# A decoder layer's seam between two attentions: the second one's first projections and norms issued in the first one's last slots

## The chip, the core and the metric

The kernel runs on one core of a Trainium2 chip. The metric is the device time in microseconds (us) of one execution of the whole program. TensorE (PE) multiplies, with PEld its weight loads; VectorE (DVE), ScalarE (ACT) and GpSimd (POOL) work on elements; SyncE (SP) issues most transfers. Each engine runs its own instructions in order, and the engines are tied together by semaphores.

## The reference

Three blocks, each followed by a norm over the 256 columns. B = 4 batches, S = 512 rows, C = 256.

```python
x = layernorm(x + attn(x))      # 16 heads of 64, softmax(q k^T / 8 + bias[bucket(k - q)]) v, then @ o_w.T
x = layernorm(x + xattn(x, ctx))
x = layernorm(x + ffn(x))       # x + sum over the 3 best of 8 zones of gelu(x @ Wa) @ Wb * w

def xattn(x, ctx):              # 16 heads of 16
    q, k, v = heads(x @ Wq + bq), heads(x @ Wk + bk), heads(x @ Wv + bv)
    y = softmax(where(causal, q k^T * scale, -inf)) v
    qc, kc, vc = heads(x @ Wcq + bcq), heads(ctx @ Wck + bck), heads(ctx @ Wcv + bcv)
    y = y + softmax(qc kc^T * scale) vc
    return y @ Wp + bp
def layernorm(x): return (x - mean(x)) / sqrt(var(x) + eps)
```

## The kernel before

Most products are made of two float16 halves of each factor (xhi + xlo, whi + wlo), as three products that add up in one bank: high by high, low by high, high by low. So every projected or turned matrix leaves its bank twice: ScalarE writes the high half and VectorE subtracts it from the bank for the low half.

**attention_1** works on 32 units u, a pair of heads of one batch each (8 pairs, 4 batches, the batch outermost). It is written as a pipeline of slots t = 0..36, each with four quarters i = 0..3. In slot t unit t is projected (project_qk, project_v, lines 371 and 381), unit t−1's row maxima are taken (line 394 on TensorE, 686 on VectorE), unit t−2's and t−3's scores are made (416, 417), get their position bias from VectorE (695) and their exponential from ScalarE (574), and are multiplied by v (426). GpSimd adds the exponentials up (768) and splits the sums (low_sum, 773); TensorE sums them over the rows (sums, 441). Unit t−4 is projected out, a quarter of the rows at a time (project_out, 458): VectorE adds the first head's part to x_acc (add_out, 715), ScalarE weighs the second head's (weigh, 595), and GpSimd adds that (add_out, 780). project_out of the next quarter waits for VectorE's addition and ScalarE's weighing. In slots 6 and 10 ScalarE and VectorE also split weights of the second attention (524 and 653). In slot 35 TensorE turns the four contexts (turn_context, 467), and in slot 36 the normalised batch 0 (turn_first, 475).

**The norm** is the class Norm: statistics (lines 140 to 145, VectorE), root (150, ScalarE, which needs a table load), even (155 to 160, VectorE: reciprocal, shift and tiles 0 and 2) and odd (166, ScalarE: tiles 1 and 3). For batch 0 it runs in slots 34 and 35, for the others in the second attention.

**attention_2** has 16 units of four heads (4 groups, 4 batches) of both the causal and the cross attention. Its order is a clock n, with tables that say at which n a unit's step stands: unit u's maxima at n = 16 + 16u + i (i = 0..15), scores from 38, values products (pv) on even n from 42, and so on. The steps overlap: at one n the maxima of one unit, the scores of the one ahead, the pv of another and the projections of the next are issued. Before the change the clock starts at n = −16. A unit's q and k (self), and on even u the cross q and on odd u the cross k for a pair of units, are projected into bank_a (line 914), in two halves on two neighbouring steps:

```python
u, i = unit_at(n, CROSS, 2)          # CROSS = -12: i = 4 and 5 of the unit whose maxima are taken
if u is not None and (u % 2 == 0 or i == 0):
    project_cross(u, i)
u, i = unit_at(n, SELF, 2)           # SELF = -5: i = 11 and 12
if u is not None:
    project_self(u, i)
```

ScalarE (high_self, high_cross) and VectorE (low_self 1177, low_cross 1183) write the halves, SyncE stores them to HBM and moves them back in eight transfers (901 to 907), so that each head lies in its place in q and k. VectorE takes the maxima from two banks (1194), four reductions to a step, and TensorE fills the banks (990, 996), scores (1020) and pv (1038). Norms and turns of batches 1 to 3 and the value products of all batches (VALUES) stand at n = −11 to 27.

## Time and profile before

| | us |
|---|---|
| median of three runs | 1324.45 |
| the three runs | 1322.35 to 1327.92 |
| the profiled execution | 1322.84 |
| its span | 1321.1 |
| mean granted TensorE clock | 0.965 |

| engine | busy us | share of the span |
|---|---|---|
| TensorE | 1182.4 | 89% |
| VectorE | 915.6 | 69% |
| ScalarE | 830.9 | 63% |
| GpSimd | 479.5 | 36% |

The busy shares are means over stages. attention_1 ends at about 566 us, attention_2's projections and norms of the first unit fill the time to 598, its units follow up to about 980, and the third block closes the span. The granted clock is a share of full speed.

### The profile page before, as it was taken

Reading aid. Unit: us, or ns where it says so; the run is one execution under the profiler, and the core shown is the slowest. Engines: PE = TensorE matmul, PEld = TensorE weight load, DVE = VectorE, ACT = ScalarE, POOL = GpSimd, SP = SyncE. Lnnn points to the kernel's source line nnn. Section 1 sums busy time; section 2 is a strip of 40 time slices with the busy share of each in tenths; the row PEclk is TensorE's granted clock in tenths of the full one; section 3 lists DMA queues with packets and bytes.
Section 4 is the critical chain, followed back from the end, with each engine's and each line's share of the span. In section 5 each row is a group of like instructions: output and inputs, shape, how many; then the busy total and the mean of one; then the engine's idle time right before and its main releaser. Section 6 shows DMA issues by size and latency. Waiting matters only on the chain. (4 is left out here: it accounts for less than half of the span.)

```text
span 1321.1 us, 25115 instructions
## 1 busy us (share of the span) xinstructions
PE 1182.4 (89%) x8862; PEld 549.9 (42%) x8862; DVE 915.6 (69%) x2346; ACT 830.9 (63%) x1587; POOL 479.5 (36%) x511
## 2 busy tenths in 40 slices
PE   6799999999999999768988888988887279999998
PEld 2343434444444444243222232222225246666666
DVE  3777777777777777557787888878842765656564
ACT  3566666666666666542667677677773476666663
POOL 0267777788888878821111111111220000000000
PEclk9999999999999999888799999999999689999999
DMA  7543324323332232011211211212100083232100
GB/s 218 164 119 100 99 77 116 83 82 82 82 91 79 78 84 57 2 54 55 70 52 41 73 50 51 72 47 67 33 2 0 5 316 121 87 128 82 63 17 16
DMA packets 82482, 103.00 MB, mean 78 GB/s; under 512 B 12626, under 2 KB 74066, under 8 KB 82326
## 3 DMA queue, kind: packets, MB, share of 16 engines
q1 hardware_dynamic: 81334, 101.26, 26.0%
q8 instruction: 71, 1.16, 0.4%
q14 instruction: 53, 0.43, 0.1%
q0 software_dynamic: 1024, 0.13, 0.1%
HBM read 65.37 MB, written 10.68 MB: 58 GB/s over the span
## 5 line engine op out<-in xcount | busy, mean ns | idle before, releaser
L1194 DVE TENSOR_REDUCE a_mx<-a_m 128x1 f32<-128x512 f32 (+3 forms) x512 | 269.0, 583 | 71.0 <-PE a_m L990 63.0
L1128 ACT ACTIVATE a_pt<-a_s 128x512 f32<-128x512 f32 (+3 forms) x512 | 235.3, 515 | 85.5 <-PE a_s L1020 82.4
L574 ACT ACTIVATE a_pt<-a_s 128x512 f32<-128x512 f32 x256 | 149.5, 597 | 164.6 <-DVE a_s L695 137.8
L990 PE MATMUL a_m<-a_k,a_q 48*128 48x512 f16 (+3 forms) x512 | 128.7, 356 | 45.6 <-DVE a_mx L1194 42.9
L686 DVE CUSTOM_DVE_ANT_0 a_junk<-a_m,a_rtile 128x512 f16<-128x512 f32 x256 | 167.3, 687 | 0.7 <-issue 0.7
L768 POOL TENSOR_TENSOR a_ps<-a_ps,a_pt 128x512 f32<-128x512 f32 x128 | 159.8, 1271 | 0.4 <-ACT a_pt L574 0.4
L426 PE MATMUL a_o<-a_pt,a_v 128*64 128x512 f32 x512 | 138.1, 617 | 2.6 <-DVE a_a L700 2.5
L695 DVE TENSOR_TENSOR a_s<-a_s,a_near 128x218 f32<-128x218 f32 (+1 forms) x256 | 108.0, 433 | 14.4 <-PE a_s L417 11.4
L1252 POOL TENSOR_SCALAR_AFFINE_SELECT a_pt<-a_pt 128x512 f32<-128x512 f32 x64 | 40.8, 637 | 210.3 <-ACT a_pt L1128 210.3
L1038 PE MATMUL a_o<-a_pt,a_v 128*17 128x512 f32 (+3 forms) x1024 | 116.4, 527 | 0.0
L1020 PE MATMUL a_s<-a_q,a_k 49*128 49x512 f16 (+3 forms) x512 | 112.8, 349 | 4.0 <-ACT a_pt L1128 3.6
L990 PEld LDWEIGHTS a_m<-a_k,a_q 48*128 48x128 f16 x512 | 35.7, 94 | 191.6 <-DVE a_mx L1194 155.3
L1555 ACT ACTIVATE ex_h<-ex_up 128x512 f32<-128x512 f32 x96 | 57.5, 599 | 81.5 <-PE ex_up L1512 81.5
L780 POOL TENSOR_TENSOR x_acc<-x_acc,a_part 128x256 f32<-128x256 f32 x128 | 93.2, 728 | 38.2 <-DVE x_acc L715 33.7
L416 PE MATMUL a_s<-a_q,a_k 128*128 128x512 f16 x256 | 98.8, 386 | 7.7 <-ACT a_pt L574 6.2
L1526 PE MATMUL ex_down<-ex_whi,ex_hh 128*128 128x256 f16 x384 | 104.7, 273 | 0.1
L1526 PE MATMUL ex_down<-ex_wlo,ex_hh 128*128 128x256 f16 x384 | 104.7, 273 | 0.0
L1526 PE MATMUL ex_down<-ex_whi,ex_hl 128*128 128x256 f16 x384 | 104.7, 273 | 0.0
L675 DVE TENSOR_TENSOR a_nat<-a_a,a_nat 128x512 f16<-128x512 f32 x64 | 44.3, 692 | 85.8 <-ACT a_nat L549 85.8
L768 POOL TENSOR_TENSOR a_ps<-a_pt 128x512 f32<-128x512 f32 x64 | 80.0, 1271 | 58.0 <-ACT a_pt L574 58.0
L417 PE MATMUL a_s<-a_q,a_k 74*128 74x512 f16 x256 | 97.6, 381 | 0.0
L773 POOL TENSOR_TENSOR a_psh<-a_ps,a_psh 128x512 f16<-128x512 f32 x64 | 72.8, 1158 | 67.5 <-ACT a_psh L580 67.5
(218 smaller groups left out, 2433.3 us busy)
## 6 DMA issues: line engine op xcount, KB each, us to landing
a_rtile<-lines SPq DMA_DIRECT2D x32, 448.0 KB, 3.9
a_q<-a_nat SPq DMA_DIRECT2D x192, 64.0 KB
a_k<-a_nat SPq DMA_DIRECT2D x192, 64.0 KB
ex_raw<-in_Wa SPq DMA_DIRECT2D x12, 1024.0 KB, 5.0
ex_raw<-in_Wb SPq DMA_DIRECT2D x12, 1024.0 KB, 7.3
halves<-a_natc SPq DMA_DIRECT2D x32, 128.0 KB, 2.4
halves<-a_nat SPq DMA_DIRECT2D x16, 256.0 KB, 2.1
a_q<-halves SPq DMA_DIRECT2D x32, 128.0 KB, 2.7
```

The costliest lines, as they stand in the source:

```text
L416: pe.matmul(bank_s[h][:, :], k1[c][:, h, ks], q1[c][:, h, ::-1], start=True, stop=False)
L426: mm = pe.matmul(bank_o[h * D1:(h + 1) * D1, :], v[u % 3][:, kb, h * D1:(h + 1) * D1], pt[:, (8 * u + 2 * kb + h) % RING, :], start=kb == ...
L574: act.activation(pt[:, n % RING, ::-1], bank_s[j % 2][:, :], ACT.Exp, scale=SC1 / QS).then_inc(sm["act_s"], 1)
L686: dve.tensor_tensor_reduce(junk[h][:, :], bank_m[h][:, :], rtile[:, u % 3, h, qb * P:qb * P + S], 1.0, -3e38, ALU.add, ALU.max, mx[u % 2][ ...
L695: dve.tensor_tensor(bank_s[h][:, first:end], bank_s[h][:, first:end], near[:, u % PAIRS * 2 + h, at:at + end - first], ALU.add).then_inc(s ...
L768: pool.tensor_tensor(ps[h][:, :], pt[:, (8 * u + h) % RING, :] if kb == 1 else ps[h][:, :], pt[:, (8 * u + 2 * kb + h) % RING, :], ALU.add ...
L990: mm[h] = pe.matmul(bank_m[j % 3][:, 0:keys], q[u % 3][o:o + ROW_M, pair, x, qb * P:(qb + 1) * P], k[u % 3][o:o + ROW_M, pair, x, 0:keys], ...
L1020: pe.matmul(bank_s[(32 * u + j) % 3][:, first:], k[u % 3][o:o + ROWS, h // 2, x, kb * P:(kb + 1) * P], q[u % 3][o:o + ROWS, h // 2, x, fir ...
L1038: mm = pe.matmul(bank_o[h * 2 * D2:h * 2 * D2 + D2 + 1, first:], v[u // GROUPS][:, x * NT + kb, u % GROUPS * G2 + h, :], pt[g % 4][:, h, f ...
L1128: act.activation(pt[g % 4][:, h, first:], bank_s[(32 * u + j) % 3][:, first:], ACT.Exp, scale=SC2 / QS).then_inc(sm["act_s"], 1)
L1194: dve.tensor_reduce(mx[u % 2][:, qb, to:to + 1], bank_m[j % 3][:, 0:keys], AX.X, ALU.max).then_inc(sm["dve_b"], 1)
L1526: mm = pe.matmul(down[t][:, :], a[k][:, f, tok], w[k][:, HALF + f * C:HALF + (f + 1) * C], start=i == 0, stop=i == len(steps) - 1)
```

## The change

- **Norms of batches 0 to 2.** Their statistics are taken by VectorE in slots 28, 29 and 30 (third quarter), one Sqrt for all three by ScalarE at the end of slot 30, between two table loads (Sqrt's and back to Exp's), and even and odd of batch b in slot 31 + b (second quarter). Batch 3 is normalised as the first thing in attention_2.
- **The bridge.** Thirteen steps e = 0..12 rotate over three banks (the two of the maxima and bank_a), at quarters that the table TURNS gives: turns of batch 0 (e = 0, 1), context of batch 0 (2), the self, cross query and cross key projections of the first unit (3, 4, 5), the other contexts (6 to 8), turns of batches 1 and 2 (9 to 12). Each is TensorE's products or transposes, ScalarE's high half, VectorE's low half (after a projection also a small memset). SyncE stores and moves the first unit's heads at the end of attention_1. Their room is a new buffer, a2_early, which attention_1 uses for wlo until its last projection.
- **The last additions.** For units 30 and 31 VectorE makes both additions of project_out from the banks (814 and 819), so ScalarE's weighing and GpSimd's addition are gone there; it also splits the sums of unit 31 (760). attention_1 has one slot fewer.
- **attention_2's clock** starts at n = 8. The value products move (the table VALUES), and the turns of batch 3 stand at n = 28, 29.
- **Projections whole.** Every projection of attention_2 is issued in one step: self at i = 10 (SELF = −6), cross at i = 4, both of them even steps, which have a pv.

```diff
-    def root(self, act, b, done):
-        act.wait_ge(self.sm["var"], done + 1)
-        act.activation(self.rs[:, 1, b * NT:(b + 1) * NT], self.rs[:, 0, b * NT:(b + 1) * NT], ACT.Sqrt).then_inc(self.sm["root"], 1)
-    def even(self, dve, b, done):
+    def root(self, act, first, end):
+        own = slice(first * NT, end * NT)
+        act.wait_ge(self.sm["var"], end)
...
+        act.activation(self.rs[:, 1, own], self.rs[:, 0, own], ACT.Sqrt).then_inc(self.sm["root"], end - first)
...
+        self.early = ctx.enter_context(nc.sbuf_tensor("a2_early", [P, 12 * S], F16))
+        self.nat, self.natc = (self.early[:, i * 2 * S:(i + 1) * 2 * S].rearrange("p (i s) -> p i s", i=2) for i in range(2))
+        self.q0, self.k0 = (self.early[:, i * 4 * S:(i + 1) * 4 * S].rearrange("p (h x s) -> p h x s", h=2, x=2) for i in (1, 2))
...
-        bank_c = [*bank_s, *bank_m]
-        bank_x = [bank_a, bank_s[0]]
+        bank_br = [*bank_m, bank_a]
         UNITS = PAIRS * B
-        SLOTS = UNITS + 5
+        SLOTS = UNITS + 4
+        LAST = UNITS - 2
+        TURNS = {(33, 0): (0, 1), (33, 1): (2,), (33, 2): (3,), (33, 3): (4,), (34, 0): (5,), (34, 1): (6,), (34, 2): (7,),
+                 (34, 3): (8,), (35, 0): (9,), (35, 1): (10,), (35, 2): (11,), (35, 3): (12,)}
+        CONTEXT, SELF2, QUERIES2, KEYS2 = {2: 0, 6: 1, 7: 2, 8: 3}, 3, 4, 5
+        TURN2 = {0: (0, 0), 1: (0, 1), 9: (1, 0), 10: (1, 1), 11: (2, 0), 12: (2, 1)}
...
+            def store_and_move(sp):
+                sp.wait_ge(second.sm["dve_self"], 1)
+                store_self(sp, second, halves2, 0)
+                sp.wait_ge(second.sm["dve_cross"], 1)
+                store_cross(sp, second, halves2, 0, second.natc)
+                sp.wait_ge(second.sm["dve_cross"], 2)
+                store_cross(sp, second, halves2, 1, natk)
+                sp.wait_ge(second.sm["st_self"], DMA)
+                sp.wait_ge(second.sm["st_cross"], 4 * DMA)
+                sp.wait_ge(sm["pe_a"], 3 * UNITS)
+                move_heads(sp, second, halves2, 0, second.q0, second.k0)
...
+                if u < UNITS - 1:
+                    pe.wait_ge(sm["pool_lo"], 2 * u + 2)
+                else:
+                    pe.wait_ge(sm["dve_lo"], 2)
...
+            def bridge(e):
+                to = bank_br[e % 3]
+                if e < 2:
+                    pe.wait_ge(sm["dve_b"], 8 * UNITS)
+                elif e == 2:
+                    pe.wait_ge(sm["act_rows"], 2 * UNITS)
+                else:
+                    pe.wait_ge(sm["dve_br"], e - 2)
+                if e in TURN2:
+                    b, k = TURN2[e]
+                    norm.ready(pe, b + 1)
+                    for n in range(NT):
+                        o = (b * NT + n) * C + k * P
+                        mm = pe.transpose(to[:, n * P:(n + 1) * P], x_acc[:, o:o + P], ident[:, :])
+                elif e in CONTEXT:
+                    pe.wait_ge(sm["ld_ctx"], DMA)
+                    for n in range(NT):
+                        mm = pe.transpose(to[:, n * P:(n + 1) * P], craw[:, CONTEXT[e] * NT + n, :], ident[:, :])
+                elif e == KEYS2:
+                    pe.wait_ge(sm["dve_br"], 3)
+                    o = CK_AT
+                    mm = product(pe, to[:, :], [(second.whi[:, o:o + P], second.wlo[:, o:o + P], second.chi[:, 0:S], second.clo[:, 0:S])])
+                else:
+                    pe.wait_ge(sm["dve_br"], 2)
+                    at = [QK_AT + c * GROUPS * P if e == SELF2 else CQ_AT + c * C for c in range(KC)]
+                    mm = product(pe, to[:, :], [(second.whi[:, o:o + P], second.wlo[:, o:o + P], xhi[:, c, 0:S], xlo[:, c, 0:S])
+                                                for c, o in enumerate(at)])
+                mm.then_inc(sm["pe_br"], 1)
...
-                    if t == SLOTS - 2:
-                        turn_context(i)
-                    if t == SLOTS - 1 and i < KC:
-                        turn_first(i)
+                    for e in TURNS.get((t, i), ()):
+                        bridge(e)
...
+                    act.wait_ge(sm["pe_a"], 3 * UNITS)
+                    to, o = {SELF2: (second.nat, 0), QUERIES2: (second.natc, GROUPS), KEYS2: (natk, GROUPS + GROUPS // 2)}[e]
+                    act.activation(to[:, 0, :], frm, ACT.Identity, bias=second.bias[:, o:o + 1]).then_inc(sm["act_br"], 1)
...
-                    if 0 <= t - 4 < UNITS:
+                    if 0 <= t - 4 < LAST:
                         weigh(t - 4, i)
                     if t in (6, 10) and i == 1:
                         split_w2(t // 10)
-                    if t == SLOTS - 2:
-                        high_context(i)
-                        if i == 0:
-                            norm.root(act, 0, 0)
-                        if i == 1:
-                            norm.odd(act, 0, 0)
-                    if t == SLOTS - 1 and i < KC:
-                        high_first(i)
+                    if (t, i) == (30, 3):
+                        norm.root(act, 0, 3)
+                    if t > 30 and t < 34 and i == 1:
+                        norm.odd(act, t - 31)
+                    for e in TURNS.get((t, i), ()):
+                        bridge(e)
...
+                    dve.scalar_tensor_tensor(to[:, 1, :], frm, second.bias[:, o:o + 1], to[:, 0, :], ALU.add, ALU.subtract
+                                             ).then_inc(done, 1)
+                    dve.wait_ge(done, 2 if e == KEYS2 else 1)
+                    dve.memset(carrier[:, 0:1], 0.0).then_inc(sm["dve_br"], 1)
+            def low_sum(h):
+                dve.wait_ge(sm["act_ps"], 2 * UNITS - 1 + h)
+                dve.tensor_tensor(psh[h][:, 1, :], ps[h][:, :], psh[h][:, 0, :], ALU.subtract).then_inc(sm["dve_lo"], 1)
...
+                if u >= LAST:
+                    dve.wait_ge(sm["pe_e1"], 4 * u + qb + 1)
+                    dve.wait_ge(sm["dve_x"], 4 * u + qb + 1)
+                    dve.scalar_tensor_tensor(x_acc[:, o:o + C], bank_e[1][:, 0:C], r[u % 2][:, 1, qb:qb + 1], x_acc[:, o:o + C],
+                                             ALU.mult, ALU.add).then_inc(sm["dve_e1"], 1)
...
-                    if t == SLOTS - 3 and i == NT - 1:
-                        norm.statistics(dve, 0, 0)
-                    if t == SLOTS - 2:
-                        if i == 1:
-                            norm.even(dve, 0, 0)
-                        low_context(i)
-                    if t == SLOTS - 1 and i < KC:
-                        low_first(i)
+                    if (t, i) == (UNITS + 2, 2):
+                        low_sum(0)
+                        low_sum(1)
+                    if 28 <= t < 31 and i == 2:
+                        dve.wait_ge(sm["pool_x"], 4 * PAIRS * (t - 27))
+                        norm.statistics(dve, t - 28)
+                    if 31 <= t < 34 and i == 1:
+                        norm.even(dve, t - 31)
+                    for e in TURNS.get((t, i), ()):
+                        bridge(e)
...
-                    if 0 <= u < UNITS:
+                    if 0 <= u < LAST:
...
-                    if i == 2 and 0 <= t - 3 < UNITS:
+                    if i == 2 and 0 <= t - 3 < UNITS - 1:
...
-        CLOCK = range(-SLOT, SLOT * (UNITS + 4) + 1)
-        CROSS, SELF, MAX, ROWS_AT, SCORE, VALUE, COPY, TURN, ADD = -12, -5, 16, 33, 38, 42, (49, 57), (56, 63), 64
-        NORM, TURN_X = (None, -2, 2, 6), (None, (5, 6), (12, 13), (18, 19))
-        VALUES = (-11, -10, -5, -4), (7, 8, 9, 11), (14, 15, 16, 17), (21, 23, 25, 27)
+        CLOCK = range(SLOT // 2, SLOT * (UNITS + 4) + 1)
+        CROSS, SELF, MAX, ROWS_AT, SCORE, VALUE, COPY, TURN, ADD = -12, -6, 16, 33, 38, 42, (49, 57), (56, 63), 64
+        TURN_LAST, VALUES = (28, 29), ((8, 9, 17, 18), (19, 20, 21, 22), (23, 24, 25, 27), (31, 33, 35, 37))
...
+                xs, at = slice(b * S, (b + 1) * S), [QK_AT + (c * GROUPS + g) * P for c in range(KC)]
+                product(pe, bank_a[:, :], [(whi[:, o:o + P], wlo[:, o:o + P], xhi[:, c, xs], xlo[:, c, xs])
+                                           for c, o in enumerate(at)]).then_inc(sm["pe_self"], 1)
...
-                u, i = unit_at(n, CROSS, 2)
-                if u is not None and (u % 2 == 0 or i == 0):
-                    project_cross(u, i)
-                u, i = unit_at(n, SELF, 2)
-                if u is not None:
-                    project_self(u, i)
+                u, i = unit_at(n, CROSS)
+                if u is not None and u > 1:
+                    project_cross(u)
+                u, i = unit_at(n, SELF)
+                if u is not None and u > 0:
+                    project_self(u)
...
+            norm.root(act, B - 1, B)
+            norm.odd(act, B - 1)
...
+            norm.statistics(dve, B - 1)
+            norm.even(dve, B - 1)
...
-                for b in range(1, B):
-                    if n == NORM[b]:
-                        norm.statistics(dve, b, b)
-                    if n == NORM[b] + 2:
-                        norm.even(dve, b, b)
-                    if n in TURN_X[b]:
-                        low_x(b, TURN_X[b].index(n))
+                if n in TURN_LAST:
+                    low_last(TURN_LAST.index(n))
```

What this does to the order, at three places. First, VectorE in slot 30, third quarter. L715 (before) and L814 (after) are add_out, L695 and L792 the bias additions that the exponentials wait for. Before:

```order
L686 ISA a_mx 128x1
L715 SCALAR_TENSOR_TENSOR x_acc<-a_e,a_r,x_acc 128x256
L695 TENSOR_TENSOR a_s<-a_s,a_near 128x308 x2
L685 MEMSET a_carrier 1x1
L686 ISA a_junk,a_mx<-a_m,a_rtile 128x512
L686 ISA a_mx 128x1
```

After:

```order
L783 ISA a_mx 128x1
L814 SCALAR_TENSOR_TENSOR x_acc<-a_e,a_r,x_acc 128x256
L140 BN_STATS n_st<-x_acc 128x6 x4
L143 BN_AGGR n_mv<-n_st 128x2 x4
L145 TENSOR_SCALAR n_rs<-n_mv 128x4
L792 TENSOR_TENSOR a_s<-a_s,a_near 128x308 x2
L782 MEMSET a_carrier 1x1
L783 ISA a_junk,a_mx<-a_m,a_rtile 128x512
L783 ISA a_mx 128x1
```

The statistics of batch 2 stand ahead of two bias additions; those of batches 0 and 1 stand alike in slots 28 and 29.

At the same slot's end, ScalarE. L574 and L660 are the exponentials, L562 and L648 copies of row maxima, L595 and L681 weigh, L587 the high half of pv. Before:

```order
L595 ACTIVATE a_part<-a_e,a_r 128x256
L574 ACTIVATE a_pt<-a_s 128x512 x2
L562 ACTIVATE a_q<-a_a 2x512 x2
L595 ACTIVATE a_part<-a_e,a_r 128x256
L574 ACTIVATE a_pt<-a_s 128x512
L549 ACTIVATE a_nat<-a_a 128x512
L574 ACTIVATE a_pt<-a_s 128x512
L595 ACTIVATE a_part<-a_e,a_r 128x256
L587 ACTIVATE a_a<-a_o 128x512
```

After:

```order
L681 ACTIVATE a_part<-a_e,a_r 128x256
L152 ACT_TABLE_LOAD
L152 ACTIVATE n_rs<-n_rs 128x12
L660 ACT_TABLE_LOAD
L660 ACTIVATE a_pt<-a_s 128x512 x2
L648 ACTIVATE a_q<-a_a 2x512 x2
L681 ACTIVATE a_part<-a_e,a_r 128x256
L660 ACTIVATE a_pt<-a_s 128x512
L635 ACTIVATE a_nat<-a_a 128x512
L660 ACTIVATE a_pt<-a_s 128x512
L681 ACTIVATE a_part<-a_e,a_r 128x256
L169 ACTIVATE x_acc<-x_acc,n_rs 128x256 x2
```

Between a weighing and the next exponentials come a table load, the root of 12 columns and a second load; in slot 31 odd stands ahead of the high half of pv.

Second, VectorE in the second half of slot 34. Before, L700 is the low half of pv and L707 the reciprocal of the sums:

```order
L715 SCALAR_TENSOR_TENSOR x_acc<-a_e,a_r,x_acc 128x256 x2
L700 SCALAR_TENSOR_TENSOR a_a<-a_o,a_a 128x512
L715 SCALAR_TENSOR_TENSOR x_acc<-a_e,a_r,x_acc 128x256 x2
L140 BN_STATS n_st<-x_acc 128x6 x4
L143 BN_AGGR n_mv<-n_st 128x2 x4
L145 TENSOR_SCALAR n_rs<-n_mv 128x4
L707 RECIPROCAL a_r<-a_e 128x8
L715 SCALAR_TENSOR_TENSOR x_acc<-a_e,a_r,x_acc 128x256
L659 TENSOR_TENSOR a_clo<-a_s,a_chi 128x512
L715 SCALAR_TENSOR_TENSOR x_acc<-a_e,a_r,x_acc 128x256
```

After, L749 is the low half of a context, L760 the split of the sums, L797 the low half of pv:

```order
L749 TENSOR_TENSOR a_clo<-a_m,a_chi 128x512
L797 SCALAR_TENSOR_TENSOR a_a<-a_o,a_a 128x512
L814 SCALAR_TENSOR_TENSOR x_acc<-a_e,a_r,x_acc 128x256
L819 SCALAR_TENSOR_TENSOR x_acc<-a_e,a_r,x_acc 128x256
L760 TENSOR_TENSOR a_psh<-a_ps,a_psh 128x512 x2
L749 TENSOR_TENSOR a_clo<-a_m,a_chi 128x512
L814 SCALAR_TENSOR_TENSOR x_acc<-a_e,a_r,x_acc 128x256
L819 SCALAR_TENSOR_TENSOR x_acc<-a_e,a_r,x_acc 128x256
L749 TENSOR_TENSOR a_clo<-a_a,a_chi 128x512
L804 RECIPROCAL a_r<-a_e 128x8
L814 SCALAR_TENSOR_TENSOR x_acc<-a_e,a_r,x_acc 128x256
L819 SCALAR_TENSOR_TENSOR x_acc<-a_e,a_r,x_acc 128x256
```

The statistics of batch 0 are gone; second additions (L819), the split of the sums and contexts stand between the additions.

Third, TensorE in a steady unit of attention_2, steps 10 to 12 of a unit's maxima (L990 and L1064 maxima, L1020 and L1094 scores, L1038 and L1112 pv, L914 and L203 projections). Before:

```order
L990 MATMUL a_m<-a_k,a_q 128x512 x2
L1020 MATMUL a_s<-a_q,a_k 128x256 x2
L914 MATMUL a_a<-xhi,a_whi 128x512
L914 MATMUL a_a<-xhi,a_wlo 128x512
L914 MATMUL a_a<-xlo,a_whi 128x512
L990 MATMUL a_m<-a_k,a_q 128x512 x2
L996 MATMUL a_m<-a_tri_q,a_identm 128x128 x4
L1020 MATMUL a_s<-a_q,a_k 128x128 x2
L914 MATMUL a_a<-xhi,a_whi 128x512
L914 MATMUL a_a<-xhi,a_wlo 128x512
L914 MATMUL a_a<-xlo,a_whi 128x512
L1038 MATMUL a_o<-a_pt,a_v 17x384 x4
```

After:

```order
L1064 MATMUL a_m<-a_k,a_q 128x512 x2
L1094 MATMUL a_s<-a_early 128x384 x2
L1064 MATMUL a_m<-a_k,a_q 128x384 x2
L1070 MATMUL a_m<-a_tri_q,a_identm 128x128 x4
L1094 MATMUL a_s<-a_early 128x256 x2
L203 MATMUL a_a<-xhi,a_whi 128x512
L203 MATMUL a_a<-xhi,a_wlo 128x512
L203 MATMUL a_a<-xlo,a_whi 128x512
L203 MATMUL a_a<-xhi,a_whi 128x512
L203 MATMUL a_a<-xhi,a_wlo 128x512
L203 MATMUL a_a<-xlo,a_whi 128x512
L1112 MATMUL a_o<-a_pt,a_v 17x512 x4
```

The six products now stand together in step 10, ahead of its pv.

## Rows read from the trace of the kernel before

**Rows 1.** Windows: start:end, length, busy by engine, PEclk, DMA share, GB/s.

```profile
445.00:460.00 15.00, 14.98 (x119) 6.55 (x119) 11.86 (x40) 9.93 (x20) 11.91 (x12) 1.00 0.30 86
530.31:542.27 11.96, 10.60 (x76) 3.66 (x75) 5.79 (x15) 8.54 (x17) 11.95 (x13) 1.00 0.01 2
542.27:554.00 11.73, 5.56 (x66) 2.45 (x64) 4.70 (x12) 4.73 (x9) 11.73 (x13) 0.83 0.00 1
566.20:597.70 31.50, 20.48 (x133) 14.65 (x133) 14.87 (x48) 14.48 (x27) 8.48 (x8) 0.84 0.25 71
597.70:620.70 23.00, 19.39 (x139) 9.64 (x139) 19.22 (x38) 6.16 (x10) 2.35 (x1) 0.95 0.21 59
620.70:636.00 15.30, 13.62 (x71) 4.23 (x71) 11.84 (x25) 7.35 (x15) 2.48 (x4) 0.52 0.16 44
692.25:715.93 23.68, 21.18 (x188) 6.91 (x192) 19.35 (x40) 17.18 (x37) 4.33 (x7) 1.00 0.19 56
929.06:950.48 21.42, 18.44 (x176) 6.28 (x180) 17.84 (x38) 16.03 (x35) 4.33 (x7) 1.00 0.13 39
```

**Rows 2.** Timeline at the seam: start, us, engine line op, [idle before <-releaser].

```profile
589.57 0.61 SPq L901 DMA_DIRECT2D a_q<-halves  x1
598.09 0.49 DVE L1194 TENSOR_REDUCE a_mx<-a_m 128x1 f32<-128x128 f32 x2 [4.15 <-PE a_m L996]
...
620.53 0.18 DVE L1201 TENSOR_SCALAR a_mx<-a_mx 128x32 f16<-128x32 f32 x1
```

**Rows 3.** Timeline: the statistics of batch 1, and TensorE in a full slot.

```profile
574.37 1.39 DVE L140 BATCH_NORM_STATS2 n_st<-x_acc 128x6 f32<-128x256 f32 x4
...
576.07 0.17 DVE L145 TENSOR_SCALAR n_rs<-n_mv 128x4 f32<-128x4 f32 x1
...
470.60 0.10 PEld L416 LDWEIGHTS a_s<-a_q,a_k 128*128 128x128 f16 x1 [0.39 <-ACT a_pt L574]
```

**Rows 4.** Timeline: starts of slots 5, 6 and 7, and the insertions of slot 6.

```profile
93.28 0.60 PE L403 MATMUL a_a<-ident,a_mx 128*2 128x128 f32 x4
...
108.82 0.60 PE L403 MATMUL a_a<-ident,a_mx 128*2 128x128 f32 x4
...
126.53 0.60 PE L403 MATMUL a_a<-ident,a_mx 128*2 128x128 f32 x4
...
116.12 1.27 ACT L524 ACTIVATE a_whi<-a_wost 128x1280 f16<-128x1280 f32 x1
117.43 1.58 DVE L653 SCALAR_TENSOR_TENSOR a_wlo<-a_wost,a_whi 128x1280 f16<-128x1280 f32 x1 [0.64 <-ACT a_whi L524]
```

**Rows 5.** Timeline: a table load, and the same operations beside GpSimd and alone.

```profile
557.33 1.28 ACT L150 ACT_TABLE_LOAD   x1
...
559.16 1.15 DVE L160 TENSOR_SCALAR x_acc<-x_acc,n_mv,n_rs 128x256 f32<-128x256 f32 x2
559.27 0.87 POOL L780 TENSOR_TENSOR x_acc<-x_acc,a_part 128x256 f32<-128x256 f32 x1 [2.27 <-ACT a_part L595]
...
576.81 0.73 DVE L160 TENSOR_SCALAR x_acc<-x_acc,n_mv,n_rs 128x256 f32<-128x256 f32 x2
...
583.46 2.35 POOL L1246 TENSOR_TENSOR x_acc<-x_acc,a_bp 128x1024 f32<-128x1024 f32 x1 [8.56 <-DVE xlo L1173]
...
585.00 0.82 DVE L145 TENSOR_SCALAR n_rs<-n_mv 128x4 f32<-128x4 f32 x1
```

**Rows 6.** Timeline: the end of the first attention.

```profile
550.95 2.27 POOL L773 TENSOR_TENSOR a_psh<-a_ps,a_psh 128x512 f16<-128x512 f32 x2
551.45 0.13 PEld L458 LDWEIGHTS a_e<-a_wohi,a_a 64*128 64x128 f16 x2 [4.97 <-issue]
...
557.37 1.11 PE L467 MATMUL a_s<-ident,a_wost 128*128 128x128 f32 x4
```

**Rows 7.** Timeline: VectorE beside projections in a steady unit.

```profile
731.90 2.59 DVE L1194 TENSOR_REDUCE a_mx<-a_m 128x1 f32<-128x512 f32 x4 [0.43 <-PE a_m L990]
...
746.83 2.06 DVE L1194 TENSOR_REDUCE a_mx<-a_m 128x1 f32<-128x512 f32 x4 [1.50 <-PE a_m L990]
```

269 lines of the change are left out of this document (133 added, 136 removed).

## The prediction

> **What bounds the kernel now.** I read the stretches of the span first [rows 1], then the timeline at the seam between the two attentions [rows 2], then the insides of three loops. The seam is the weak place. From 566.20 to 597.70 us TensorE is busy 20.48 us of 31.50 and VectorE 14.87; everything there prepares the second attention. Its first maximum is taken at 598.09 [rows 2]. What sets the length is a chain: normalise, turn, project, store, move into the heads' places (the first move is issued at 589.57), multiply. Ahead of it the first attention runs out: in 542.27–554.00 GpSimd is busy 11.73 of 11.73 us while TensorE is busy 5.56. Both loops beside the seam are tight. A full slot of the first attention has TensorE busy 14.98 of 15.00 us. A unit of the second takes 23.68 us with projections in it and 21.42 without; TensorE and VectorE hand over to each other there.
>
> The profiled execution took 1322.84 us, 1.6 below the median of the three runs (1324.45); the three differ by 5.6. I sum against 1322.84 and give the result as it is. A measurement can tell 0.5%, 6.6 us, from no change.
>
> **Part 1, the seam shrinks: −24.6 us.** Before, 598.09 − 566.20 = 31.9 us lie between the first attention's end and the first maximum. After, the first unit's projections, stores and moves have been issued in slots 33 to 35, so the eight moves (0.61 us of SyncE each, by the row at 589.57) lie beside the last four project_out steps. Left at the seam are the statistics of batch 3 at 1.9 (576.24 − 574.37, [rows 3]), the load of Sqrt's table at 1.3 (557.33) and VectorE's two halves of the norm at 0.7 (576.81, [rows 5]), together 3.9, and, at an estimate of mine of 3.4, the clearing of a bank, Sqrt, reciprocal, shift, one conversion and four hand-overs between engines. That is 7.3 us. 31.9 − 7.3 = 24.6.
>
> **Part 2, the first unit's maxima grow: +2.8.** They took 620.53 − 598.09 = 22.4 us. The clock now begins at n=8, and value products that ran in the seam come beside them: those of the context of batch 0 (n=17, 18), all of batch 1 (19–22) and the first two of batch 2, while three of batch 3 move out behind. A full-width product takes TensorE 0.23 us: the unit with projections has 12 more of them than the one without (188 against 176) and 21.18 − 18.44 = 2.74 us more [rows 1]. A value product as wide as six of them is 1.4 us, one of the context 0.7. Added: 1.4 (the two of batch 0's context) + 4.2 (batch 1) + 2.8 (batch 2), less 2.8 (batch 3) = 5.6 us of TensorE. It was busy 19.39 of 23.00 us; 3.6 us of idle take what they can, but only in the steps where it is idle. In steps 17 to 27 I count 17.1 us of TensorE against some 14 of VectorE, so +2.8, with ends 2.0 (all idle used) and 5.6 (none).
>
> **Part 3, insertions in slots 28 to 32: +9.6.** The full loop hides nothing of what is put in front of the bias additions: at 470.60 TensorE's load waits 0.39 us for ScalarE's exponential (line 574), which follows VectorE's bias addition (line 695) [rows 3]. The one precedent is slot 6, where ScalarE got 1.27 us and VectorE, behind it, 1.58 us [rows 4]: from one set of rows to the next the slot took 126.53 − 108.82 = 17.71 us, the one ahead of it 108.82 − 93.28 = 15.54; so 2.17 of 2.85 us came through, 0.76 of each. The statistics stand ahead of two bias additions in three slots, 1.9 us each: 3 × 1.9 × 0.76 = 4.3. The Sqrt in slot 30 needs two table loads, 2 × 1.28 = 2.6 us [rows 5], with the root some 2.8, on ScalarE between exponentials: 2.8 × 0.76 = 2.1. The first norm halves (slot 31) put 1.15 us (559.16, [rows 5]) and two small operations on VectorE and about as much on ScalarE ahead of high_o: like slot 6, 2.1. Those of slot 32 come where the last unit is already projected: 1.1. Ends: 2.5 (hidden but for the table loads) and 11.7 (all of it through).
>
> **Part 4, slots 33 to the end: +3.3.** Slot 33 gets three turns of four transposes, 1.11 us each by the one at 557.37 [rows 6], and two whole products at 1.4, 6.1 us of TensorE; it was busy 10.60 of 11.96 [rows 1], so +4.7. In slot 34 GpSimd was the bound. It ends with the low sums (2.27 us at 550.95, [rows 6]) for which TensorE's load stood idle 4.97 us. VectorE takes these and GpSimd's last eight additions; to its 4.70 us come four contexts or halves, four second additions and the two low sums, in all some 11 of 11.7 us: 0. In slot 35 each project_out is followed by two additions, not one, but the turns of batches 1 and 2 wait for none of them, where before the turns of batch 0 stood behind the last addition: −1.4, of the 12.2 us from 554.0 to 566.2. Ends: −2 and +7.
>
> **Part 5, steady units: +10.2.** This part is small in the diff and large in the sum. Before, the six products of a projection are issued in halves on two neighbouring steps; now all stand in one, an even step that also holds the value products of a quarter. The rows show what one half does. In step 11, the odd one, VectorE idles 0.43 us (731.90). In the first even step of the cross projection, where one half stands before the change too, VectorE then idles 1.50 us (746.83) [rows 7]. A second half there adds 3 × 0.23 = 0.7 us of idle, since TensorE can't reach the next maxima. What the odd step gives back is at most its 0.43. I take +0.6 for the self product in twelve units and +0.5 for the cross product in six even ones: 7.2 + 3.0. Ends: 0 and 14.
>
> VectorE's conversions and SyncE's stores of these projections are the same in number and a step earlier; nobody waits for them for another five steps, so nothing.
>
> **Part 6, the clock: −1.** TensorE was granted 0.84 of its clock in the seam and 0.52 in the first 15 us of the second unit, beside 1.00 in the full loops [rows 1]. With less idling there I give back 1 us.
>
> **Sum:** −24.6 + 2.8 + 9.6 + 3.3 + 10.2 − 1.0 = +0.3, so **1323 us**. The bounds of the terms give 1316 to 1331 for this case if not all miss in one direction.
>
> **Weighed against a rule.** At 559.16 VectorE's two tensor_scalar halves took 1.15 us beside an addition of GpSimd; at 576.81 the same took 0.73. At 585.00 one of 4 columns took 0.82 instead of 0.17, while GpSimd ran an addition of 1024 columns [rows 5]. The Trainium skill, "SBUF — State Buffer", section "Who interferes with whom", says that VectorE in its two-port mode and GpSimd take turns at a shared port pair and that the later one stands fully blocked. These rows fit that rule. With it the moved operations would pay as much again beside a busy GpSimd, 3.2 us by (d) below; without it nothing, and the sum stands.
>
> **Rivals.**
> (a) *Steady units don't feel part 5.* For: VectorE idles at even steps already, and the odd step is freed. Against: 746.83. Then 1323 − 10 = **1313**.
> (b) *Slots 28–32 absorb the insertions*, since VectorE is busy only 11.86 us of 15.00 and ScalarE 9.93. Against: slot 6. Then 1323 − 7 = **1316**; with (a), **1306**.
> (c) *The slow clock falls on the full unit*, the case slower than before. From 620.7 to 636.0 TensorE ran at about half its clock (0.52, [rows 1]; the lower level, 1.2 GHz), in a unit that had room. If this stretch comes in the first unit, where after the change TensorE is the bound, 15.3 us at half do 7.6 us of work less, and part 2's +2.8 doubles. 1323 + 10.4 = **1333**. It decides once TensorE has work for more than half of the stretch; with 17.1 us of it in steps 17 to 27 it has.
> (d) *Blocked VectorE.* GpSimd is busy 11.91 of 15.00 us in the slots that get the statistics. Three small operations at +0.65 and three norm halves at +0.42: +3.2, **1326**. The skill's rule above is this case.
> (e) *The seam doesn't shrink as said*, because the stores and moves queue at the end of SyncE's list until the last conversions are through and the first maximum waits for them: 8 us of moves come back, **1331**.
>
> **How the numbers follow.** The forecast has 0.42, (a) 0.18, (b) alone 0.12, (a) with (b) 0.06, (c) 0.12, (d) 0.06, (e) 0.04. Faster by over 0.5%, below 1317.8, are most of (a) and (b), both together and the lower edge of the forecast: 0.14 + 0.07 + 0.06 + 0.05 = 0.32. Slower by over 0.5%, above 1331.1, are (c), half of (e) and the upper edge: 0.12 + 0.02 + 0.05 = 0.19. Within: 0.49. The range from 1308 to 1334 leaves out some 2 in 10: most of (a) with (b), and what lies above (c). The likeliest case's own is 1316 to 1331.
>
> **What would show it.** Part 1: the first maximum 7 to 8 us behind the last conversion of the first attention, no idling for moves in front of it. Part 2: the first unit's 32 maxima in 25 us, VectorE idle behind TensorE. Part 3: slots 28 to 30 at 16.4 us, 31 near 17, against 15.0. Part 4: slot 33 at 16 us. Part 5: steady units with projections at 24.3 to 24.8 us instead of 23.68, units without at 21.4; longer idling of VectorE in the even step of the projection. I am wrong if units stay at 23.7 (then (a)), if slots 28 to 32 stay at 15 (then (b)), or if the granted clock is 0.5 between n=16 and n=32 (then (c)).

## The result: 1.75% slower, and where the time went

The changed kernel takes 1348.74 us (median of 4 runs, 1346.82 to 1349.13) beside 1325.14 for the kernel before in the same comparison: ratio 1.0175, 95% interval 1.0151 to 1.0199. 1323 was forecast, with a range to 1334. Its profiled execution took 1348.67 us, span 1346.7, 25.6 longer than the 1321.1 of before.

The same marks, read in both traces, give the whole difference. TensorE's turning of the row maxima (the rows of [rows 4]; line 466 after) marks the start of a slot, and the scaling of the maxima ([rows 2], 620.53) marks a unit's end.

| stretch | before | after | difference | forecast |
|---|---|---|---|---|
| slots 28, 29, 30 | 15.55, 15.56, 15.54 | 17.66, 18.87, 17.67 | +7.6 | +4.3 |
| slot 31 | 15.56 | 21.18 | +5.6 | +4.2 (with the root) |
| slot 32 | 12.60 | 17.70 | +5.1 | +1.1 |
| slot 33 to the first maximum | 67.8 | 48.2 | −19.6 | −21.3 |
| first unit's maxima | 22.4 | 24.5 | +2.0 | +2.8 |
| second and third unit | 22.6, 25.6 | 26.45, 24.85 | +3.1 | 0 |
| units 4 to 14 | 23.55 and 23.68 in turn (one of 24.35) | 25.25 and 26.0 in turn | +20.9 | +10.2 |
| last two units | 21.4 | 21.4 | 0 | 0 |
| the rest (start −1.1, third block +2.0) | | | +0.9 | −1 (clock) |

The seam did what was said of it. What was paid for it was twice what was said, in the two loops beside it.

The page of the profile after: its head, the clock over the span, and the group of the maxima. The last line is the same group on the page before.

```profile
span 1346.7 us, 25074 instructions
PE 1196.4 (89%) x8862; PEld 556.4 (41%) x8862; DVE 921.4 (68%) x2359; ACT 826.3 (61%) x1579; POOL 471.2 (35%) x501
...
PEclk9999999999999999878998998998998679999999
...
L1268 DVE TENSOR_REDUCE a_mx<-a_m 128x1 f32<-128x512 f32 (+3 forms) x512 | 268.2, 584 | 93.3 <-PE a_m L1064 87.5
L1194 DVE TENSOR_REDUCE a_mx<-a_m 128x1 f32<-128x512 f32 (+3 forms) x512 | 269.0, 583 | 71.0 <-PE a_m L990 63.0
```

VectorE reduces in the same time as before, but idles 93.3 us in front of it where it idled 71.0. And the line of the granted clock has an 8 at regular distances through the units from some 660 us on, where before it was all 9. Windows of the kernel after, columns as in [rows 1]: the five slots, two units, and two short stretches, each across the end of a unit.

```profile
454.40:472.10 17.70, 15.74 (x122) 6.67 (x121) 13.97 (x50) 10.27 (x20) 13.24 (x14) 1.00 0.32 92
472.10:490.90 18.80, 16.87 (x121) 6.96 (x120) 13.87 (x50) 10.27 (x20) 12.46 (x12) 0.91 0.27 75
490.90:508.60 17.70, 15.73 (x121) 6.65 (x120) 13.97 (x50) 10.38 (x21) 12.55 (x13) 1.00 0.28 70
508.60:529.80 21.20, 17.41 (x121) 7.01 (x120) 13.22 (x45) 14.04 (x25) 11.77 (x12) 0.92 0.16 41
529.80:547.50 17.70, 14.58 (x86) 4.54 (x85) 13.26 (x43) 9.72 (x20) 14.33 (x15) 0.81 0.01 2
...
722.50:747.70 25.20, 21.98 (x194) 7.59 (x197) 19.33 (x39) 17.19 (x38) 4.31 (x7) 0.95 0.19 54
747.70:773.70 26.00, 22.36 (x176) 7.46 (x176) 19.35 (x39) 16.86 (x37) 4.31 (x7) 0.91 0.19 52
...
718.00:725.50 7.50, 7.16 (x54) 2.68 (x54) 5.61 (x13) 4.14 (x9) 0.86 (x2) 0.54 0.10 35
768.70:776.20 7.50, 6.63 (x46) 2.28 (x45) 5.61 (x13) 3.59 (x7) 1.36 (x2) 0.54 0.10 35
```

The second unit row is a unit of the same kind as that of 692.25 in [rows 1], and VectorE is busy 19.35 us in both: the same work, 26.0 us instead of 23.68. Once in every pair of units TensorE runs some 7 us at half its clock (0.54 in the mean, 0.50 inside: 1.2 GHz). Before, the row of 692.25 had 1.00.

Where a unit waits, VectorE's timeline in the unit from 747.7 to 773.7 tells, to be laid beside [rows 7]; the first row here is one more of the kernel before, its step 12:

```profile
758.78 1.29 DVE L1194 TENSOR_REDUCE a_mx<-a_m 128x1 f32<-128x512 f32 x2 [0.61 <-PE a_m L990]
...
755.71 1.95 DVE L1268 TENSOR_REDUCE a_mx<-a_m 128x1 f32<-128x512 f32 x4 [2.15 <-PE a_m L1064]
...
765.74 2.53 DVE L1268 TENSOR_REDUCE a_mx<-a_m 128x1 f32<-128x512 f32 x4 [1.83 <-PE a_m L1064]
```

2.15 us behind the cross product, 1.50 before. 1.83 us behind the self product, for which step 11 and step 12 had 0.43 and 0.61 before, together 1.04. TensorE's timeline around the second shows six products in a row (the first and the last are given), the value products behind them, and the steps after:

```profile
762.93 0.39 PE L203 MATMUL a_a<-xhi,a_whi 128*128 128x512 f16 x1
...
764.02 0.38 PE L203 MATMUL a_a<-xlo,a_whi 128*128 128x512 f16 x1
764.33 1.05 PE L1112 MATMUL a_o<-a_pt,a_v 128*17 128x512 f32 x8
765.32 0.39 PE L1064 MATMUL a_m<-a_early 48*128 48x512 f16 x2
...
766.49 0.39 PE L1064 MATMUL a_m<-a_early 48*128 48x512 f16 x1 [0.46 <-DVE a_mx L1268]
...
769.58 0.60 PE L1064 MATMUL a_m<-a_early 48*128 48x512 f16 x1 [0.87 <-DVE a_mx L1268]
```

The same form of product takes 0.39 us at 766.49 and 0.60 at 769.58: between them TensorE had little to do, in part none (0.46 and 0.87 us idle, where the projection's second half used to stand), and its clock had fallen.

### The profile page after: what moved, and what is told of

Its sections match the earlier page's. It is cut to its first block and busy times, and to the rows that moved or that the text cites. A ratio compares the mean times of both kernels' runs of the same rounds, so it can differ in the third digit from the quotient of the medians.

```text
span 1346.7 us, 25074 instructions
## 1 busy us (share of the span) xinstructions
PE 1196.4 (89%) x8862; PEld 556.4 (41%) x8862; DVE 921.4 (68%) x2359; ACT 826.3 (61%) x1579; POOL 471.2 (35%) x501
## 3 DMA queue, kind: packets, MB, share of 16 engines
q1 hardware_dynamic: 81334, 101.26, 25.5%
## 5 line engine op out<-in xcount | busy, mean ns | idle before, releaser
L1268 DVE TENSOR_REDUCE a_mx<-a_m 128x1 f32<-128x512 f32 (+3 forms) x512 | 268.2, 584 | 93.3 <-PE a_m L1064 87.5
L660 ACT ACTIVATE a_pt<-a_s 128x512 f32<-128x512 f32 x256 | 149.5, 597 | 177.3 <-DVE a_s L792 152.4
L489 PE MATMUL a_o<-a_pt,a_v 128*64 128x512 f32 x512 | 141.1, 630 | 8.0 <-DVE a_a L797 8.0
L792 DVE TENSOR_TENSOR a_s<-a_s,a_near 128x218 f32<-128x218 f32 (+1 forms) x256 | 107.6, 433 | 17.2 <-PE a_s L480 14.2
L1112 PE MATMUL a_o<-a_pt,a_v 128*17 128x512 f32 (+3 forms) x1024 | 118.6, 537 | 0.0
L1064 PE MATMUL a_m<-a_k,a_q 48*128 48x512 f16 (+3 forms) x320 | 81.9, 363 | 32.1 <-DVE a_mx L1268 30.7
L886 POOL TENSOR_TENSOR x_acc<-x_acc,a_part 128x256 f32<-128x256 f32 x120 | 87.1, 725 | 46.3 <-DVE x_acc L814 36.2
L1668 DVE SCALAR_TENSOR_TENSOR x_acc<-ex_down,wbc,x_acc 128x256 f32<-128x256 f32 x48 | 23.2, 484 | 91.8 <-PE ex_down L1596 91.6
L1582 PE MATMUL ex_up<-xhi,ex_whi 128*128 128x512 f16 x192 | 73.6, 383 | 12.8 <-DVE ex_wlo L1656 12.8
```

Source lines behind the costliest of these rows:

```text
L489: mm = pe.matmul(bank_o[h * D1:(h + 1) * D1, :], v[u % 3][:, kb, h * D1:(h + 1) * D1], pt[:, (8 * u + 2 * kb + h) % RING, :], start=kb == ...
L660: act.activation(pt[:, n % RING, ::-1], bank_s[j % 2][:, :], ACT.Exp, scale=SC1 / QS).then_inc(sm["act_s"], 1)
L792: dve.tensor_tensor(bank_s[h][:, first:end], bank_s[h][:, first:end], near[:, u % PAIRS * 2 + h, at:at + end - first], ALU.add).then_inc(s ...
L1112: mm = pe.matmul(bank_o[h * 2 * D2:h * 2 * D2 + D2 + 1, first:], v[u // GROUPS][:, x * NT + kb, u % GROUPS * G2 + h, :], pt[g % 4][:, h, f ...
L1268: dve.tensor_reduce(mx[u % 2][:, qb, to:to + 1], bank_m[j % 3][:, 0:keys], AX.X, ALU.max).then_inc(sm["dve_b"], 1)
L1582: mm = pe.matmul(up[f % 4][:, :], w[k][:, c * FF + f * P:c * FF + (f + 1) * P], m[:, c, xs], start=i == 0, stop=i == len(steps) - 1)
```

## The experiments

### Part 5: undone, done alone, and taken apart

**e1** undoes the whole projections in the changed kernel and nothing else.

```diff
-        CROSS, SELF, ... = -12, -6, ...
+        CROSS, SELF, ... = -12, -5, ...
...
-                u, i = unit_at(n, SELF)
+                u, i = unit_at(n, SELF, 2)
...
-                    project_self(u)
+                    project_self(u, i)          # three of the six products each; cross likewise
```

> The changed kernel, but every projection of the second attention is again issued in two halves on two neighbouring steps (self at steps 11 and 12, cross at 4 and 5); all else stays. Theory W (the whole products in an even step cost 1.5 to 2.4 us a unit, as waits of VectorE and as a clock that falls once in two units): units with projections return from 25.25 and 26.0 to 23.6 us, granted clock 1.00 in them, 22 to 24 us less than the changed kernel in all: about 1325 us. Theory S (the units are slower for what the change did ahead of them, for instance moved value products or buffers): units stay at 25 to 26, time near 1348.

Measured: 1323.42 us, ratio 0.9996 (0.9979 to 1.0014). Units 4 to 14 take 23.55 and 23.68 us in turn, as before to a hundredth. **e2** does this part alone in the kernel before.

```diff
-        CROSS, SELF, ... = -12, -5, ...
+        CROSS, SELF, ... = -12, -6, ...
...
-                    project_self(u, i)
+                    for c in range(KC):
+                        project_self(u, c)      # both halves in one step; cross likewise
```

> The kernel before, with nothing changed but that projections are issued whole at even steps (self at 10, cross at 4). Theory W: units of 25.25 and 26.0 us in turn, 22 to 25 us slower than before, about 1348 us. Theory S: at most 3 us slower.

Measured: 1349.52 us, ratio 1.0216 (1.0168 to 1.0265), units of 25.24 and 25.99 us in turn (but the fourth, 24.22). So this part costs some 25 us in either kernel, 20 to 21 of them in units 4 to 14, and everything else of the change taken together costs nothing and brings nothing (e1). Theory S is out.

**e5** has only the cross projection whole, **e7** only the self projection. **e6** has both whole, but a step later, on odd steps (`CROSS, SELF = -11, -5`).

> The changed kernel with the self projection back in two halves (steps 11 and 12); the cross projection stays whole at step 4. In a pair of units the waits of part 5 are, by the rows of both traces, 0.65 us for the cross product and 2 x 0.8 for the two self products, and the slow clock 1.8. If each wait stands for itself and the clock falls only for both: pair 47.9 us, granted clock 1.00, about 1327 us. If the clock falls for the cross product's idling alone: pair 49.7, 1339 us.

> The changed kernel with the cross projection back in halves; the self projection stays whole at step 10. Waits alone: pair 47.2 + 1.6 = 48.8 us, 1334 us. With the slow clock as well: pair 50.6 us, 1345 us.

> The changed kernel with its projections whole, but at odd steps, which have no value products beside them (self at 11, cross at 5). If it is the neighbourhood of the value products that costs: pair 47.2 to 48 us as in halves, about 1324 to 1328 us. If a block of six products costs wherever it stands: pair 49 to 51 us, 1335 to 1347 us.

Two neighbouring units of each, windows with the columns of [rows 1]. e5:

```profile
698.30:722.50 24.20, 21.24 (x188) 7.18 (x192) 19.31 (x39) 17.17 (x37) 4.31 (x7) 1.00 0.20 55
722.50:746.10 23.60, 20.64 (x185) 6.93 (x189) 19.34 (x40) 17.18 (x38) 4.31 (x7) 1.00 0.20 58
```

e7:

```profile
675.70:701.00 25.30, 22.07 (x197) 7.63 (x197) 19.42 (x40) 17.25 (x39) 4.31 (x7) 0.95 0.19 54
701.00:725.30 24.30, 21.11 (x188) 7.05 (x184) 19.20 (x39) 17.03 (x37) 4.32 (x7) 1.00 0.19 55
```

e6:

```profile
694.20:718.50 24.30, 21.21 (x189) 7.11 (x192) 19.27 (x40) 17.01 (x37) 4.33 (x7) 1.00 0.19 55
718.50:742.20 23.70, 20.61 (x187) 6.86 (x189) 19.30 (x40) 17.02 (x38) 4.33 (x7) 1.00 0.20 57
```

e5 took 1328.17 us (ratio 1.0027, 1.0015 to 1.0040): its units are 23.55 and 24.20 us in turn, so the pair is 0.53 us longer than in e1, and the clock stays at 1.00. e7, of which there are only two executions, took 1344.94 (1.0159, 1.0132 to 1.0186). Its units are 24.2 to 25.5 us, in the mean 24.96 (11 units from 675.7 to 950.3) against 23.61, and every 75 us, once in three units, the clock falls to 0.50. The unit between two falls, the second row of e7 above, runs at 1.00 and takes 24.35 us (the others of this kind 24.23 and 24.36), 0.67 longer than its like in e1. e6 took 1330.85 (1.0055, 1.0035 to 1.0074), with units of 23.63 and 24.28 us at a clock of 1.00, pairs of 47.9 us.

That takes the changed kernel's 4.0 us a pair apart: 0.53 for the cross product (e5), 2 × 0.67 for the two self products (e7, at full clock), and the rest, 2.1, goes with the slow clock. e7 gives the same 2.1 for each of its falls: three units take 74.96 us, three at the full clock would take 72.9. The last term is a remainder in both, but the waits are now measured without a fall beside them.

The same six products in one block cost 0.7 us a pair at odd steps and 4.0 at even ones. The cross product has no part in that: 0.53 either way. The self product costs 0.67 a unit at the even step and 0.08 at the odd one, and with it goes the fall of the clock. What differs is what TensorE does between two fillings of the maxima's banks: after, the six products and eight value products, 2.39 us (762.93 to 765.32 above); in e6 the six alone, 1.40 us:

```profile
734.65 0.39 PE L203 MATMUL a_a<-xhi,a_whi 128*128 128x512 f16 x1
...
736.05 0.39 PE L1064 MATMUL a_m<-a_k,a_q 48*128 48x512 f16 x2
```

That the value products beside the block are the cause is the reading that fits; no kernel has the block at an even step without them.

### Part 3: doses

**e3** adds the statistics of batches 0 to 2 to the kernel before, in the same places, into buffers that nobody reads. **e4** adds one Sqrt of 12 columns at the end of slot 30.

```diff
+                    if 28 <= t < 31 and i == 2:
...
+                        extra_statistics(t - 28)
```
```diff
+                    if (t, i) == (30, 3):
+                        act.activation(xrs[:, :], ident[:, 0:12], ACT.Sqrt).then_inc(sm["xr"], 1)
```

> The kernel before, with the statistics of batches 0 to 2 taken once more in slots 28, 29 and 30, into buffers that nobody reads, where the changed kernel takes them. Theory F (all that is put ahead of two bias additions comes through, and TensorE's idling then lets its clock fall): slots 28 to 30 take 17.7, 18.9 and 17.7 us instead of 15.55, 7 to 8 us slower in all. Theory P (the prediction, 0.76 of each): 16.9 to 17.0 us each, 4.3 us in all. In both the slots behind stay as they are.

> The kernel before, with one Sqrt of 12 columns and so two table loads added on ScalarE at the end of slot 30, result unread. Theory F: 2.8 us come through whole and slot 31 loses some 1 us more to the clock, 3 to 4.5 us slower. Theory P: 2.1 us. If a switch of tables costs 2.66 us and not the 1.28 that the load's row shows: 5.5 us or more.

e3 took 1330.06 us (1.0057, 1.0036 to 1.0078), and slots 28 to 30 17.67, 17.67 and 17.66 us. Three times 2.12 us come through, all of the operations, as theory F had it; the fall of the clock that it added for slot 29 did not come. In the changed kernel VectorE's timeline shows what they are made of and who pays:

```profile
467.30 1.39 DVE L140 BATCH_NORM_STATS2 n_st<-x_acc 128x6 f32<-128x256 f32 x4
468.61 0.36 DVE L143 BATCH_NORM_AGGREGATE n_mv<-n_st 128x2 f32<-128x6 f32 x4
469.00 0.50 DVE L145 TENSOR_SCALAR n_rs<-n_mv 128x4 f32<-128x4 f32 x1
469.42 0.86 DVE L792 TENSOR_TENSOR a_s<-a_s,a_near 128x308 f32<-128x308 f32 x2
...
470.66 0.39 PE L479 MATMUL a_s<-a_q,a_k 128*128 128x512 f16 x1 [1.57 <-ACT a_pt L660]
471.64 0.39 PE L479 MATMUL a_s<-a_q,a_k 128*128 128x512 f16 x1 [0.37 <-ACT a_pt L660]
```

From 467.30 to 469.42 are 2.12 us, and TensorE idles 1.57 + 0.37 of them. (The small operation on four columns takes 0.50 us here, 0.17 where GpSimd is idle, [rows 3].) The slow clock of slot 29, 1.2 us, came in the changed kernel, in e6 and in e7, and not in e1, e3 or e5, which have the same slots: it goes with the idling but not each time (the window of 472.10 above has 0.91).

e4 took 1325.15 us (1.0025, 1.0007 to 1.0043), an interval that holds both theories. The slot decides: slot 31 is 19.25 us instead of 15.55, +3.7, at a granted clock of 0.91 where it was 1.00, so a part of the 3.7 is the clock's. ScalarE's timeline of e4, then TensorE's:

```profile
502.58 1.28 ACT L631 ACT_TABLE_LOAD   x1
503.87 0.21 ACT L631 ACTIVATE a_xrs<-ident 128x12 f32<-128x12 f32 x1
504.10 1.28 ACT L575 ACT_TABLE_LOAD   x1
505.39 1.09 ACT L575 ACTIVATE a_pt<-a_s 128x512 f32<-128x512 f32 x2
506.50 1.06 ACT L563 ACTIVATE a_q<-a_a 2x512 f16<-2x512 f32 x2
...
507.67 0.38 PE L417 MATMUL a_s<-a_q,a_k 128*128 128x512 f16 x1 [2.13 <-ACT a_q L563]
```

From 502.58 to 505.39 are 2.81 us: the two switches cost their loads and no more. The Trainium skill, "ScalarE: Activation LUTs", section "What ACT_TABLE_LOAD costs", gives 1283 ns for the load, as these rows do, and with a drain 2.66 us for each switch; the drain isn't in these rows, where the root starts 0.01 us behind its load. But behind the loads stand two exponentials and the copy of the row maxima (line 563), for which TensorE waits 2.13 us.

### The place instead of the work

**e8** is e1 with the statistics where VectorE idles: bn_stats in the second quarter ahead of the projection's low half, the aggregation in the third.

```diff
+                    if 28 <= t < 31 and i == 1:
...
+                        norm.collect(dve, t - 28)
+                    if 28 <= t < 31 and i == 2:
+                        norm.aggregate(dve, t - 28)
                     if t < UNITS and 0 < i < 3:
                         low(t, i - 1)
...
-                        norm.statistics(dve, t - 28)
```

> e1 (all projections in halves), and besides the statistics in slots 28 to 30 no longer stand ahead of two bias additions in the third quarter: the four bn_stats stand in the second quarter ahead of the projection's low half, for which VectorE idles 1.53 us, and the aggregation in the third ahead of the other low half (1.24 us idle). If it was the place and not the work that cost: slots 28 to 30 back to 15.6 us, 6.4 us less than e1, about 1317 us. If VectorE's work costs anywhere: as e1, 1323 us.

Measured 1317.95 us (0.9963, 0.9943 to 0.9984), and its slot 28 is

```profile
454.70:470.20 15.50, 15.48 (x121) 6.65 (x120) 13.56 (x50) 10.29 (x20) 12.40 (x13) 1.00 0.30 82
```

VectorE is busy 13.56 us, in the same slot before 11.9, and the slot is not longer. It wasn't VectorE's work that cost but what it stood ahead of. (In the new place the small operation on four columns takes 0.17 us again.) Slots 31 and 32 are shorter too, 20.22 and 15.67 us against 21.19 and 17.70 in e1, though nothing was moved in them; in slot 32 the granted clock is 0.89 instead of 0.81.

**e9** moves the norm's halves: odd a quarter later, even within its quarter ahead of the low half. **e10** in addition has the Sqrt behind the copy of the row maxima, and batch 0's halves a quarter later still (odd in the fourth, even in the third quarter of slot 31).

```diff
-                    if (t, i) == (30, 3):
+                    if (t, i) == (31, 0):        # e10
                         norm.root(act, 0, 3)
-                    if t > 30 and t < 34 and i == 1:
+                    if t > 30 and t < 34 and i == 2:   # e9
                         norm.odd(act, t - 31)
...
+                    if 31 <= t < 34 and i == 1:        # e9, ahead of low; taken out behind it
+                        norm.even(dve, t - 31)
```

> e8 with the norm's halves of batches 0 to 2 moved: even stands in the second quarter of slots 31 to 33 ahead of the projection's low half (or what stands there), odd behind the high half of pv at the end of the third quarter. In e8 TensorE waits 2.42 us in slot 32 for the low half of pv, which waits for odd. If the order on ScalarE is the cause: slot 32 from 15.7 to 13.5 us, slot 31 1 us shorter, in all 3 us less than e8. If the work costs anywhere: as e8, 1318 us.

> e9 with the Sqrt and its two table loads one quarter later, behind the copy of the row maxima in slot 31 (TensorE waits 2.13 us for that copy in e8), and the norm halves of batch 0 one quarter later each. If the copy is what made the root dear: slot 31 from 20.2 us (e8) to 17.5, 2 us less than e9. If ScalarE's time costs anywhere in a full slot: as e9.

e9 took 1315.48 us (0.9942, 0.9923 to 0.9960): slot 31 fell from 20.2 to 18.9 us, slot 32 stayed at 15.6, and from slot 33 to the first maximum it is 51.1 us, where e8 had 46.9. That was a miss: even now stood between the two bias additions of slot 32. e10 took 1311.74 (0.9928, 0.9902 to 0.9954), with slot 31 at 17.06 and without TensorE's wait of 2.13 us for the copy. The slot is 1.9 us shorter than in e9, but two things were moved, the root and batch 0's halves, and the runs don't part them. In e10's slot 32 the price of the misplaced half is to be seen, on VectorE, GpSimd and TensorE:

```profile
524.34 2.70 DVE L169 TENSOR_SCALAR x_acc<-x_acc,n_mv,n_rs 128x256 f32<-128x256 f32 x2
524.36 2.53 POOL L882 TENSOR_TENSOR a_ps<-a_ps,a_pt 128x512 f32<-128x512 f32 x2
...
528.11 0.39 PE L485 MATMUL a_s<-a_q,a_k 128*128 128x512 f16 x1 [2.07 <-ACT a_pt L666]
```

The two operations of even take 0.73 us where GpSimd is idle ([rows 5], 576.81) and 2.70 here, side by side with two long additions of GpSimd. In e9's slot 31 they take 2.65, in e10's 0.73. So what stands beside an operation on GpSimd is a second price of its place, next to what stands behind it.

**e11** takes back the third part of the change: e8 with ScalarE and GpSimd making the second additions of units 30 and 31.

```diff
-        LAST = UNITS - 2
+        LAST = UNITS
```

> e8 with the last additions of units 30 and 31 back on ScalarE's weighing and GpSimd (the split of unit 31's sums stays with VectorE). If VectorE's takeover brings what it takes from GpSimd: from the last row maxima to the first maximum of the second attention 3 to 5 us more than e8 (46.9 us). If it only moves work: within 1 us of e8, or 1 us less, since weighing runs beside the first addition.

Measured 1312.59 us (0.9937, 0.9912 to 0.9961), not to be told from e8 by the time. Slot 33 to the first maximum is 45.6 us against 46.9. TensorE's project_out in the last slot, e8:

```profile
568.59 0.40 PE L532 MATMUL a_e<-a_wohi,a_a 64*128 64x256 f16 x2 [0.69 <-DVE a_r L810]
...
570.64 0.40 PE L532 MATMUL a_e<-a_wohi,a_a 64*128 64x256 f16 x2 [0.19 <-DVE x_acc L825]
...
572.94 0.28 PE L532 MATMUL a_e<-a_wohi,a_a 64*128 64x256 f16 x2 [0.43 <-DVE x_acc L825]
...
574.99 0.28 PE L532 MATMUL a_e<-a_wohi,a_a 64*128 64x256 f16 x2 [0.96 <-DVE x_acc L825]
```

and e11:

```profile
568.30 0.40 PE L532 MATMUL a_e<-a_wohi,a_a 64*128 64x256 f16 x2 [0.35 <-issue]
...
570.11 0.39 PE L532 MATMUL a_e<-a_wohi,a_a 64*128 64x256 f16 x2
...
571.99 0.36 PE L532 MATMUL a_e<-a_wohi,a_a 64*128 64x256 f16 x2
...
573.79 0.28 PE L532 MATMUL a_e<-a_wohi,a_a 64*128 64x256 f16 x2 [0.63 <-DVE x_acc L820]
```

Steps of 2.05 to 2.3 us with both additions on VectorE, of 1.8 to 1.9 with one of them weighed beside. In this stage VectorE's taking over is a small loss, 1.3 us in the profiled executions.

**e12** puts the findings together: e10 and e11, and the halves of batches 1 and 2 behind both bias additions.

> Everything that the runs so far found put together: projections in halves, statistics in VectorE's gaps, the Sqrt behind the row maxima's copy in slot 31, additions of units 30 and 31 with ScalarE and GpSimd as before, and the norm halves of batches 1 and 2 moved behind both bias additions (even at the end of slots 32 and 33, odd in the second quarter of slots 33 and 34). In e10 the even of slot 32 stood between two bias additions and TensorE waited 2.07 us. If place is what costs: slots 28 to 30 15.55, 31 17.1, 32 12.6 to 13.6 us, some 3 to 5 us less than e10 and e11, about 1308 us. If slot 32 then loses elsewhere (GpSimd's exponentials): as e10, 1312 us.

Measured 1309.89 us, ratio 0.9893 (0.9877 to 0.9910), faster than both kernels. Slots 28 to 32 take 15.54, 15.54, 15.54, 17.05 and 12.81 us: 1.7 us more than before, where the change had paid 18.3. The window of its slot 32, for the row of 529.80 above:

```profile
519.50:532.30 12.80, 11.75 (x86) 4.11 (x85) 10.80 (x40) 9.31 (x19) 11.76 (x12) 1.00 0.01 2
```

But slot 32 is short here because even now runs just behind the mark. VectorE's row, and TensorE's first project_out behind it, for which e11 idles 0.35 us:

```profile
532.33 2.16 DVE L169 TENSOR_SCALAR x_acc<-x_acc,n_mv,n_rs 128x256 f32<-128x256 f32 x2
...
535.30 0.29 PE L532 MATMUL a_e<-a_wohi,a_a 64*128 64x256 f16 x2 [2.05 <-issue]
```

From slot 33 to the first maximum e12 takes 48.45 us, e11 45.56. Slot 32 and this stretch together are 61.3 us in e12 and 61.2 in e11: moving the halves of batches 1 and 2 brought nothing that lasts. What e12 has over e11 is slot 31, 17.05 instead of 20.40. So the kernels are better laid side by side over the whole way from the start of slot 28 to the first maximum:

| | before | after | e1 | e8 | e9 | e10 | e11 | e12 |
|---|---|---|---|---|---|---|---|---|
| us | 142.6 | 141.3 | 140.1 | 129.4 | 132.2 | 129.7 | 128.2 | 124.9 |

The change brought 1.3 us on this way, the statistics in VectorE's gaps another 10.6 (e1 to e8), more than the 6.4 of the three slots. e9 is worse than e8 here and e10 is like it, and the intervals of their times overlap with that of e8, so neither is shown to be faster. Times of whole runs don't repeat these differences one for one: the third block alone took 350 us in e1's profiled execution and 357 in e8's, with no edit in it.

## Why the prediction was wrong, by its own steps

**Part 1 and part 4, right.** From slot 33 to the first maximum the sum had −24.6 + 3.3 = −21.3; −19.6 was measured. The first maximum came at 595.68 us, 7.0 behind the first operation of the second attention (588.65), and nothing idled for the moves. Inside part 4 a piece was missed: the taking over of GpSimd's last additions was put at nothing, and e11 shows a small loss.

**Part 2, right in size, short in reach.** The first unit got 2.0 us longer (2.8 forecast). But value products of batch 3 now stand in the second unit (n = 33, 35, 37), which the sum left out: 26.45 us against 22.61, +3.8, with TensorE at a clock of 0.83 (0.65 before). No run takes these products out, so that they are the cause isn't shown.

**Part 3, the mechanism right, the size half.** +9.6 was forecast, +18.3 measured. Two terms failed. The first is the factor 0.76 that was taken from slot 6. There VectorE's insertion stands behind ScalarE's, in other places of a quarter; from one such row a share was made and used everywhere. Ahead of two bias additions all of it comes through (e3: 2.12 of 2.12 us, three times, 6.4 instead of 4.3), and slot 29 lost another 1.2 with its clock. The root cost 3.7 us and not 2.1 (e4): the row maxima's copy stood behind it, and the clock fell to 0.91. What is left of slot 31, 1.9, was forecast at 2.1. The second is slot 32, put at 1.1 for the reason that the last unit is already projected, with no row. The two norm halves stand there ahead of the low half of pv, for which TensorE waits 2.42 us, and the slot cost 5.1. Some 2.0 of that went away in e8, which has the same operations in the slot and a clock of 0.89 instead of 0.81. The other 3.1 went out of the slot in e12 and came back, 2.9, behind it. (A full slot is 15.55 us long; the 15.0 that the signs were set against is the length of the window in [rows 1]. The sum doesn't use it.)

**Part 5, the waits right, the size half.** This is the largest miss, and the failed step is that the waits of VectorE were taken for the whole price. The row at 746.83 and its reading were right: 0.5 a pair was forecast for the cross product and 0.53 measured (e5), 0.6 a unit for the self product and 0.67 measured (e7). In units 4 to 14 that makes 10.1 us. But these units lost 20.9: the other 10.8, 2.1 us in each pair, go with a TensorE clock that now falls to half for 7 us, a term that the sum didn't have. Part 6 had given back 1 us for the clock, and rival (c) had looked for the slow clock in one place, the first unit, not as something that a moved product brings to every pair.

**The rivals.** (a) and (b) were both wrong, in the direction away from the truth. (c) was the right kind of loss at the wrong place: the first unit ran at the full clock for its first 20 us (1.00), and at 0.98 over the whole. (d) is there in small in the changed kernel: the norm's halves took 1.15 and 1.21 us beside GpSimd in slots 31 and 32 and 0.73 in slot 33, the operation of four columns 0.50 instead of 0.17. In e9 and e10 it is there in full, 2.65 and 2.70. (e) didn't come. The range ended at 1334, just above (c). With the upper ends of part 3 (11.7) and part 5 (14) the sum comes to 1329; both were drawn from the same rows as the terms, and neither had room for the clock.

## What to carry to other kernels

Where two engines hand banks to each other without slack, ask of each inserted operation what stands directly behind it on its own engine and who waits for that: the same statistics cost 6.4 us ahead of two bias additions and nothing a quarter earlier, the same products 4.0 us a pair in one step and 0.7 in the next. Ask as well what GpSimd does beside it: the same two operations took 0.73 us and 2.70. A part of a change that looks like tidying (two halves put into one call) can outweigh all the rest when it stands in a loop; do each part alone before the sum is believed. Where an operation is moved, read the price up to a mark that lies behind all its places: slot 32 of e12 looks 2.8 us shorter than in e11, and the way to the first maximum isn't, but for slot 31. And where a wait on TensorE grows, the clock is a second price beside the wait.

## What the runs showed of the hardware that was not expected

- The granted clock fell in a steady loop that had run at 1.00 but for one short fall (0.72 over 784 to 790 us before, ahead of and in the unit of 24.35): now once in two units, for some 7 us at half (0.54 over 7.5 us), after idle times of TensorE of 0.46 and 0.87 us around a step with little work. These idle times alone don't decide it: both kernels have the same two in every unit from the fourth to the fourteenth, and the clock falls behind every second of them after, behind every third in e7. With the cross projection alone moved (e5), or both at odd steps (e6), it stayed at 1.00 in units 4 to 14.
- The same slots with the same insertions lost their clock in some kernels (slot 29: 18.87 us after, 17.66 in e1).
- Two table loads with a root between them took 2.81 us of ScalarE in all, nothing beyond the loads and the operation.
- Two operations of VectorE on 256 columns took 2.70 us beside two additions of GpSimd on 512 columns that lasted 2.53, and 0.73 without them. The profile shows this in the operations' own duration, with no wait in front of them.
